# Graph-attention tail of a four-block graph network: target columns out of split rows, no masks under the logits, first tile's projection behind its transposition, first residual beside the last product

## The reference, cut to what matters

```python
def gat(x, src, dst, W, a_src, a_dst, bias, heads):       # one attention layer
    h = (x @ W).reshape(n, heads, -1)
    al_s = (h * a_src).sum(-1); al_d = (h * a_dst).sum(-1)
    e = leaky_relu(al_s[src] + al_d[dst], 0.2)
    e = exp(e - segment_max(e, dst)[dst])
    alpha = e / (segment_sum(e, dst)[dst] + 1e-16)
    return segment_sum(h[src] * alpha, dst) + bias
# block 3: h = relu(gat(h, 768 -> 4 heads x 64)); h = relu(gat(h, 256 -> 1 x 256)); h = relu(h @ Wm1 + bm1) @ Wm2 + bm2
# block 4: h = elu(gat(h, 768 -> 8 heads x 96)); h = gat(h, 768 -> 1 x 768)
x = x + block(relu(layernorm(x)))
```

## Time and profile before

| what | value |
|---|---|
| median of three runs (lowest, highest) | 935.74 us (931.85, 939.06) |
| the profiled execution, own time / span | 938.73 us / 936.9 us |
| mean granted TensorE clock | 0.949 of 2.4 GHz |
| PE, DVE, ACT, POOL busy (share of the span) | 837.0 (89%), 616.9 (66%), 378.4 (40%), 513.8 (55%) us |
| last product of block 2 ends / attention begins | 755.5 us / 764.2 us |
| last instruction of DVE ends | 933.8 us |

### The profile page before, as it was taken

How to read it: one execution, slowest core, us unless ns; L and a number is a source line. 1 busy time by engine, 2 the same in 40 slices (tenths; PEclk the granted TensorE clock), 3 DMA queues, 4 the chain that set the end, 5 groups by cost and what they waited for, 6 DMA issues and landing times.

```text
span 936.9 us, 10275 instructions
## 1 busy us (share of the span) xinstructions
PE 837.0 (89%) x4096; PEld 648.3 (69%) x4096; DVE 616.9 (66%) x700; ACT 378.4 (40%) x410; POOL 513.8 (55%) x225
## 2 busy tenths in 40 slices
PE   8999999998788999889886899999999957879877
PEld 3569966775456995666553699899879946545644
DVE  8955079899995319899998575465379563333442
ACT  1124276666643437667563343334333312110310
POOL 0437459999982738999996377166527600000000
PEclk9999999999999999999999899999999987568979
DMA  8046335344324634305322566176355360000000
GB/s 347 4 131 206 131 91 135 101 135 135 101 68 139 199 101 131 95 1 214 111 75 94 201 203 202 36 269 202 102 181 187 122 252 1 1 0 1 1 0 34
DMA packets 24263, 111.00 MB, mean 118 GB/s; under 512 B 3604, under 2 KB 5908, under 8 KB 23832
## 3 DMA queue, kind: packets, MB, share of 16 engines
q1 hardware_dynamic: 23096, 104.24, 34.1%
q10 hardware_dynamic: 1120, 6.10, 1.7%
HBM read 100.63 MB, written 0.79 MB: 108 GB/s over the span
## 4 chain that ended last, share of the span: by engine, by line
PE 57%; POOL 25%; DVE 12%; ACT 3%; issue 2%; DMA 1%; DVEq 0%; ACTq 0%
PE ps L955 20%; POOL prod L561 17%; PE ps L903 9%; POOL prod L564 6%; PE ps L940 6%; DVE prod L1685 5%; PE ps L1335 4%; POOL w_lo L549 3%; PE ps L1010 2%; PE ps L1394 2%; PE ps L1031 2%; PE ps L1311 2%; DVE qi_t L1703 1%; PE ps L1188 1%; PE ps L1329 1%
## 5 line engine op out<-in xcount | busy, mean ns | idle before, releaser
L549 POOL TENSOR_TENSOR w_lo<-w_raw,w_hi 128x1536 fp32r<-128x1536 f32 x54 | 197.0, 3655 | 146.6 <-ACT w_hi L615 146.5
L561 POOL TENSOR_TENSOR prod<-prod 128x1024 f32<-128x1024 f32 x94 | 226.5, 2425 | 40.6 <-DVE prod L1685 40.4
L720 ACT ACTIVATE prod<-ps 128x1024 f32<-128x1024 f32 x192 | 187.8, 1024 | 96.3 <-PE ps L1141 72.8
L1685 DVE TENSOR_TENSOR prod<-prod,ps 128x2048 f32<-128x2048 f32 x96 | 218.7, 2279 | 3.2 <-ACT prod L720 2.5
L1141 PE MATMUL ps<-sel_pair,h_and_q 128*128 128x512 f32 x384 | 130.7, 453 | 22.1 <-ACT prod L720 21.9
L903 PE MATMUL ps<-w_raw,h_t 128*128 128x384 f32 x408 | 141.8, 494 | 0.0
L615 ACT ACTIVATE w_hi<-w_raw 128x1536 fp32r<-128x1536 f32 x54 | 80.2, 1488 | 136.8 <-PE ps L955 93.7
L955 PE MATMUL ps<-w_hi,yt_hi 128*128 128x384 f32 x432 | 111.0, 337 | 5.2 <-POOL w_lo L549 5.2
L903 PEld LDWEIGHTS ps<-w_raw,h_t 128*128 128x128 f32 x408 | 78.2, 194 | 46.0 <-issue 2.6
L955 PE MATMUL ps<-w_lo,yt_hi 128*128 128x384 f32 x432 | 109.7, 334 | 0.0
L955 PE MATMUL ps<-w_hi,yt_lo 128*128 128x384 f32 x432 | 109.7, 334 | 0.0
(11 more groups left out here) (194 smaller groups left out, 1113.0 us busy)
## 6 DMA issues: line engine op xcount, KB each, us to landing
w_raw<-weights SPq DMA_DIRECT2D x105, 768.0 KB, 4.4
wa_in<-weights SPq DMA_DIRECT2D x6, 768.0 KB, 5.9
w_gat<-weights SPq DMA_DIRECT2D x6, 768.0 KB, 8.1
w_query<-weights SPq DMA_DIRECT2D x3, 768.0 KB, 11.3
h_and_q<-stage_hi SPq DMA_DIRECT2D x24, 96.0 KB, 2.1
h_and_q<-stage_lo SPq DMA_DIRECT2D x24, 96.0 KB, 2.2
a_vec<-gat_vectors ACTq DMA_DIRECT2D x1, 2048.0 KB, 8.0
q_t<-queries ACTq DMA_DIRECT2D x1, 1536.0 KB, 10.2
```

What stands on the lines that cost most here:

```text
L549: pool.tensor_tensor(Wl[:, j, :], raw_slab(U, 0, j), Wh[:, j, :], ALU.subtract).then_inc(w_lo_ready, 1)
L561: pool.tensor_tensor(v[:, :, 0:32], v[:, :, 0:32], v[:, :, 32:64], ALU.add).then_inc(folded_once, 1)
L720: act.activation(slot_view(s)[:, :, 32 * u:32 * u + 32], args.rearrange("p b (n l) -> p (b n) l", l=LH), ACT.Sigmoid).then_inc(sigmoid_rea ...
L1685: TT(slot_view(s), slot_view(s), ps[:, 6, o:o + L].unsqueeze(1).broadcast_to([P, NB, L]), ALU.mult).then_inc(products_ready, 1)
```

## The change

1. Columns: `logit_columns` no longer contracts over the input. It takes one product for each tile from the split rows AR[:,1] with a selector of 8 columns. It now waits for the rows (`g_dst_rows`) and stands behind `masked` on PE; DVE's copy of the columns still stands ahead of its maxima.
2. Masks: no `masks` in `logits`, and no table `noedge_s`. One 512-wide product and two of 256 columns fill each bank. `counted` takes the smaller of the weight and 1 before it multiplies by the count, in the same instruction.
3. Projection: `projection` of tile 0 (all of it in g = 0, two chunks in g = 2 and 3) goes right behind the transposition of tile 0, which for g = 0 and 2 stands ahead of that of tile 1. `keep_h` of tile 0 moves up on ACT. The last sums (L1526) run over tile 0 first and wait for each tile's `keep_h` by itself; target tile 1 goes to banks 6 and 7.
4. Residual: `last_residual(0)` starts at `out0_ready`. The `Wa` work of g = 0 is split around `norm_shift(2, 0)`, ahead of the residual of tile 1, and that of g = 1 goes behind the weights of g = 0 with a buffer of its own.

```diff
-            def logit_weights(g, w, k0, n, done):
+            def logit_weights(g, w, k0, n, done, vectors=(0, 1)):
...
-                tmp = wa_tmp[:, 0:width]
+                tmp = wa_tmp1[:] if g == 1 else wa_tmp[:, 0:width]
...
-            wait_landed(dve, 30, 0, 0)
-            logit_weights(0, raw_slab(30, 0, 0), 0, 6, True)
-            wait_landed(dve, 30, 0, 1)
-            logit_weights(1, raw_slab(30, 0, 1)[:, 0:2 * N], 0, 2, True)
-            for t in range(NT):
+            def last_residual(t):
                 wait_out(dve, LAYERS - 1, t)
                 residual(t, two_banks(2 * t)).then_inc(residual_added, 1)
                 dve.wait_ge(residual_added, t + 1)
                 norm_stats(2, t)
-            for t in range(NT):
-                norm_shift(2, t)
+            last_residual(0)
+            wait_landed(dve, 30, 0, 0)
+            logit_weights(0, raw_slab(30, 0, 0), 0, 6, False, (0,))
+            norm_shift(2, 0)
+            logit_weights(0, raw_slab(30, 0, 0), 0, 6, True, (1,))
+            last_residual(1)
+            norm_shift(2, 1)
...
             gat_weights(0)
+            wait_landed(dve, 30, 0, 1)
+            logit_weights(1, raw_slab(30, 0, 1)[:, 0:2 * N], 0, 2, True)
             heads_out(0, 0, 6, 1)
...
             def logit_columns(g):
-                hn, n = GAT[g][0], IN_CHUNKS[g]
+                hn = GAT[g][0]
+                pe.wait_ge(g_dst_rows, g + 1)
                 for t in range(NT):
-                    for k in range(n):
-                        ins = pe.matmul(ps[:, 6, t * hn:(t + 1) * hn], HT[:, k, t * P:(t + 1) * P],
-                                        Wa[:, WB[g] + k, 32:32 + hn], start=(k == 0), stop=(k == n - 1))
+                    ins = pe.matmul(ps[:, 6, t * SELK:(t + 1) * SELK], AR[:, 1, t * P:(t + 1) * P], selb[0:64, :, 0],
+                                    start=True, stop=True)
...
             def logits(g, u):
                 b0 = logit_bank(g, u)
-                masks(g, u, noedge_s, b0)
-                for i, (t, h) in enumerate(BLOCKS[g][u]):
-                    pe.matmul(block_of(b0, i), AR[:, 0, t * P:(t + 1) * P], selb[0:64, h, 0:1].broadcast_to([64, N]),
-                              start=False, stop=False)
-                    ins = pe.matmul(block_of(b0, i), selb[0:64, h, :], AR[:, 1, :], start=False, stop=(i % 2 == 1))
+                p = BLOCKS[g][u]
+                for b in range(len(p) // 2):
+                    both = ps[:, b0 + b, :].rearrange("p (h n) -> p h n", h=2)
+                    t, h = p[2 * b]
...
+                        pe.matmul(both, AR[:, 0, t * P:(t + 1) * P], selb[0:64, h:h + 2, 0:1].broadcast_to([64, 2, N]),
+                                  start=True, stop=False)
+                        for i in range(2):
+                            ins = pe.matmul(both[:, i, :], selb[0:64, h + i, :], AR[:, 1, :], start=False, stop=(i == 1))
...
-                    TT(w3, w3, c3, ALU.mult).then_inc(g_weights_ready, 1)
+                    dve.scalar_tensor_tensor(out=w3, in0=w3, scalar=1.0, in1=c3, op0=ALU.min,
+                                             op1=ALU.mult).then_inc(g_weights_ready, 1)
...
-            transposes(0, H, norm_h_ready, 0, 6, (4, 6))
-            masks(0, 0, noedge_d, 0)
-            wait_landed(pe, 30, 0, 2)
+            transpose_tile(0, H, norm_h_ready, 0, 6, 4)
...
+            pe.wait_ge(ht0_ready, 1)
+            pe.wait_ge(residual_added, 2)
+            projection(0, 0, 0, 6)
+            transpose_tile(1, H, norm_h_ready, 0, 6, 6)
+            masks(0, 0)
             logit_rows(0)
-            logit_columns(0)
             pe.wait_ge(g_src_rows, 1)
             masked(0, 0)
-            masks(0, 1, noedge_d, 4)
+            masks(0, 1)
             masked(0, 1)
-            projection(0, 0, 0, 6)
-            pe.wait_ge(g_dst_rows, 1)
+            logit_columns(0)
+            projection(0, 1, 0, 3)
             for u in range(2):
                 pe.wait_ge(g_masked_read, u + 1)
                 logits(0, u)
             max_rows(0)
-            projection(0, 1, 0, 6)
+            projection(0, 1, 3, 6)
...
+            transpose_tile(0, H, norm_h_ready, 2, 6, 4)
+            pe.wait_ge(ht0_ready, 4)
+            pe.wait_ge(w31_landed, 48)
+            projection(2, 0, 0, 2)
+            transpose_tile(1, H, norm_h_ready, 2, 6, 6)
+            projection(2, 0, 2, 3)
             logit_rows(2)
+            projection(2, 0, 3, 4)
+            pe.wait_ge(g_src_rows, 3)
+            masks(2, 0)
+            masked(2, 0)
             logit_columns(2)
...
             pe.wait_ge(g_cols_copied, 3)
-            pe.wait_ge(g_dst_rows, 3)
-            masks(2, 1, noedge_d, 6)
+            masks(2, 1)
             masked(2, 1)
-            projection(2, 0, 1, 3)
...
+            pe.wait_ge(ht0_ready, 5)
+            pe.wait_ge(w32_landed, 48)
+            projection(3, 0, 0, 2)
             logit_rows(3)
+            projection(3, 0, 2, 3)
+            pe.wait_ge(g_src_rows, 4)
+            masks(3, 0)
+            masked(3, 0)
             logit_columns(3)
...
-            pe.wait_ge(g_h_copied, 8)
...
-            for d in range(NT):
-                for u in range(2):
-                    for t in range(NT):
+            for t in range(NT):
+                pe.wait_ge(g_h_copied, 7 + t)
+                for d in range(NT):
+                    for u in range(2):
```

More of the change, by code:

```diff
@@ L846, in _ @@
             first_half(0, 4, 6, False)
+            keep_h(0, 0)
             target_rows(0)
@@ L1291, in _, with transpose_tile @@
                 layer_products(layer)
-            def transposes(e, src, ready, count, chunks, banks):
-                for t in range(NT):
[L1297 to L1300, removed]
+            def transpose_tile(t, src, ready, count, chunks, bank):
+                pe.wait_ge(ready, count + t + 1)
+                for k in range(chunks):
+                    ins = pe.transpose(chunk_tile(bank, chunks)[:, k, :], src[:, t, k * P:(k + 1) * P], ident[:])
+                ins.then_inc(t_done, 1)
             W30 = Wr[:, 0:3, :].rearrange("p j f -> p (j f)")
@@ L1341, in block_of, with masks @@
                 return ps[:, b0 + i // 2, (i % 2) * N:(i % 2 + 1) * N]
-            def masks(g, u, table, b0):
+            def masks(g, u):
                 p = BLOCKS[g][u]
+                b0 = piece_bank(g, u)
                 for b in range(len(p) // 2):
                     t = p[2 * b][0]
-                    both = table[:, g // 2, :, :] if len(BLOCKS[g]) == 1 else                         table[:, g // 2, t, :].unsqueeze(1).broadcast_to([P, 2, N])
+                    both = noedge_d[:, g // 2, :, :] if len(BLOCKS[g]) == 1 else \
+                        noedge_d[:, g // 2, t, :].unsqueeze(1).broadcast_to([P, 2, N])
                     pe.matmul(ps[:, b0 + b, :].rearrange("p (h n) -> p h n", h=2), identb[:], both, start=True, stop=False)
@@ L1359, in logits @@
                 b0 = logit_bank(g, u)
-                masks(g, u, noedge_s, b0)
-                for i, (t, h) in enumerate(BLOCKS[g][u]):
-                    pe.matmul(block_of(b0, i), AR[:, 0, t * P:(t + 1) * P], selb[0:64, h, 0:1].broadcast_to([64, N]),
-                              start=False, stop=False)
-                    ins = pe.matmul(block_of(b0, i), selb[0:64, h, :], AR[:, 1, :], start=False, stop=(i % 2 == 1))
+                p = BLOCKS[g][u]
+                for b in range(len(p) // 2):
+                    both = ps[:, b0 + b, :].rearrange("p (h n) -> p h n", h=2)
+                    t, h = p[2 * b]
+                    if len(BLOCKS[g]) == 1:
+                        pe.matmul(both, selb[0:64, h, :], AR[:, 1, :].unsqueeze(1).broadcast_to([64, 2, N]),
+                                  start=True, stop=False)
+                        for i in range(2):
+                            ins = pe.matmul(both[:, i, :], AR[:, 0, i * P:(i + 1) * P], selb[0:64, h, 0:1].broadcast_to([64, N]),
+                                            start=False, stop=(i == 1))
+                    else:
+                        pe.matmul(both, AR[:, 0, t * P:(t + 1) * P], selb[0:64, h:h + 2, 0:1].broadcast_to([64, 2, N]),
+                                  start=True, stop=False)
+                        for i in range(2):
+                            ins = pe.matmul(both[:, i, :], selb[0:64, h + i, :], AR[:, 1, :], start=False, stop=(i == 1))
                 ins.then_inc(g_logits_ready, 1)
@@ L1421, in _ @@
             weighted(0, 1, 0, 4, 2, True)
-            transposes(1, gout, gout_ready, 0, 2, (3, 7))
-            masks(1, 0, noedge_d, 4)
+            transpose_tile(0, gout, gout_ready, 0, 2, 3)
+            masks(1, 0)
+            transpose_tile(1, gout, gout_ready, 0, 2, 7)
             logit_rows(1)
-            logit_columns(1)
+            projection(1, 0, 0, 2)
             pe.wait_ge(g_src_rows, 2)
             masked(1, 0)
-            for t in range(NT):
-                projection(1, t, 0, 2)
```

(49 more changed lines are left out.)

24 lines of the change are left out of this document (11 added, 13 removed).

## The result

| | before | after |
|---|---|---|
| median of four runs each (lowest, highest), us | 937.4 (931.85, 940.91) | 912.51 (910.11, 913.43) |
| profiled execution, own time / span, us | 938.73 / 936.9 | 910.11 / 908.3 |
| mean granted clock | 0.949 | 0.962 |

The ratio is 0.9736, with a 95% interval of [0.9681, 0.9791]: 24.9 us less by the medians, 19.6 to 29.9 by the interval. The forecast was 914.3 us (905 to 924). One run of all that follow, 2202.39 us of the kernel wide_filler, was in a slower state and is left out.

A forecast was written before the change was run, and what follows sets the result against it. PE's order and its clock were taken as the bound in the tail. Gains of 5.2 + 1.8 + 5.7 + 8.7 = 21.4 us, taken from the median of 935.74, gave 914.3 us, with a range of 905 to 924.

The forecast's parts named there:

- Before attention: Part 4, from the last product to `h_t` of tile 0: copy ready at 764.2 us, against 766.6 before.
- two queues: Ahead of g = 0: ACT's copy queued behind tile 1's norm, and the wait for both residuals, hold the projection back.
- g = 0: First attention layer, projection to maxima: gain 5.2 us, with 1.5 us charged for one low-clock stretch.
- g = 1: Second layer: old columns and a mask bank go, against the new columns; gain 1.8 us.
- g = 2: Third layer: columns, masks, filled wait and low stretch gained, less new waits and transposition; gain 5.7 us.
- g = 3: Last layer: filled waits, columns, mask and clock; gain 8.7 us.
- The reason that was given for the low clock: Rows stretch of g = 3: transpositions don't count as PE activity; were they counted, 10.4 us instead of 8.7.
- Unseen costs: Minimum inside `counted` taken as nothing (1.8 us from above); new columns 0.25 us, from 0.12 each to 0.43 each.
- stages not touched: g = 1's weights and the two-layer network: no gain counted, low-clock share may shift 2 us either way.
- Only the removals pay: Rival, whole tail: only removed columns and masks gain, 12.5 us, or 923, and the moves cancel out; chance 0.22.
- the clock holds: Rival: low stretches behind the columns vanish and early projections raise the clock sooner; 28 us, 907; chance 0.15.
- The slower one: Rival: new waits turn high-clock stretches of g = 2 and 3 low, up to 40.8 us more, 955; chance 0.03.

The follow-up runs named there:

- wide_filler: Kernel before with only the new columns, plus as many unread 128-wide products where the old columns stood; 928.35 us, 0.992.
- early: Changed kernel with ACT's copy of tile 0 ahead of tile 1's norm and the projection of g = 0 in bank 0; 907.5 us, 0.9703.
- early_fill: As early, with one chunk of the second tile's projection in g = 2 moved ahead of `max_rows`; 905.38 us, 0.9675.
- run 12: Not a follow-up run: the words say that PE had executed 12 transpositions in g = 0; no kernel or measured time belongs to them.
- old_masks: Changed kernel with the second masks put back under the logits; 916.48 us, 0.9798.
- old_residual: Changed kernel with both residuals put back behind the logit weights of both layers; 915.7 us, 0.9773.
- old_order: Changed kernel with the old order of projections, ACT copies and last sums put back in all four layers; 916.71 us, 0.9794.
- the repeat: Changed kernel run again unchanged for a second trace; 912.69 us.

## Why the prediction was right

- **The bound.** PE's order and its clock, as read from the earlier trace rows. Shown for the columns by wide_filler: equal PE work, 6 us less.
- **The time is nearer than the gain, by luck.** 912.51 us is 1.8 us from the forecast. The gain was 24.9 us instead of 21.4, 3.5 more; the forecast started from 935.74 us, and a fourth run moved the median of the kernel before to 937.4.
- **Before attention.** Residual 0 at 749.5 us (forecast 749.4), the copy at 764.2 us (764.2), the rows of g = 0 at 773.3 us (772.9). That two queues keep the projection out of PE's idle time is shown by early, which changes both; neither was changed alone.
- **g = 0, 6.0 for 5.2 us.** The charged low stretch of 1.5 us didn't come; the path behind the rows took 9.0 us (8.9 at the high clock were worked out).
- **g = 1, 2.0 for 1.8 us**, from before traces that differ by 3 us among themselves.
- **g = 2, 5.1 for 5.7 us.** The price before `max_rows` is there: PE waits 0.83 us for DVE's late maxima (0.85 forecast), and early_fill gets 0.7 us of it back. That the moves of this stage pay is not shown: with the old order it took 32.4 us.
- **g = 3, 9.2 for 8.7 us.** The first projection ran at the low clock for 4.54 us, as taken, and all behind it at 1.00. The reason that was given for the low clock doesn't hold up in these traces. In the stretch from which it was read, PE also stood idle for 2.8 us ahead of the rows. In g = 0 the clock rose at 767.1 us, when PE had run 12 transpositions and begun a mask since 764.2 us. And the same projection behind the same transpositions ran at 1.00 in early_fill and in old_masks, where L1335 is the projection:

```profile
880.57 2.85 PE ps L1335 x8
```

So 4.54 us was one of several values that this projection took (3.41 us in early, 3.66 in old_residual), and that it came out as forecast is partly luck. The Trainium skill ("TensorE: Matmul & The Clock Gate", "Part 4: PE-mode transpose") says that a transposition doesn't count as PE activity for the clock; these traces don't bear that out for the transpositions of this kernel.

- **Unseen costs.** The minimum costs nothing: two operations in 2.36 us, like the two products of before. New columns: 0.12 us for both tiles, under the 0.25 taken. The row that the forecast called narrow (L1364) is 256 columns wide, with 64 partitions.
- **The mis-sized term** is the one set at zero: stages not touched. They gave 3.2 us of the mean gain of 25.5: 1.6 in the stage with the two-layer network, where the traces before differ by 4.4 us among themselves, and 1.6 in the sums of g = 2, repeatable and unexplained. With 22.3 us from the four touched stages the sum of 21.4 was 0.9 short.
- **The rivals.** "Only the removals pay" (923) lies 9.6 us above the slowest run, and old_order speaks against it; "the clock holds" was half true: all behind the columns, but not the first projections. The slower one never set in: over 25.4 us of g = 2 with the new waits the clock was 1.00.

## What to carry to other kernels

Very narrow products were paid twice here: 24 of them took as long as their weight loads, and what stood behind them ran at half the clock in most cases. Read the granted clock behind them before you price them by their own duration, and derive such columns from rows that are there already. Work moved into an idle stretch arrives only if every in-order queue on its way lets it pass: here ACT's norm of the other tile and one shared bank held it back until both were changed. Price low-clock stretches by stage and take more than one trace, as a stage that the change doesn't touch moved by 2 to 4 us here. Do the same for each part that is put back: a median of four runs doesn't tell 2 us of the part from 2 us of another stage, and the stages do.

## What the runs showed of the hardware that was not expected

A single-column power on POOL (L554, 128x1) takes 0.55 us alone, but 2.00 us at 752.03 us, while DVE runs the 1536-wide product L1799 (1.75 us); 1.99 us in the repeat and 2.00 in early. It is not DVE's work as such that stretches it: in the kernel before it took 0.55 us at 760.77 us, beside DVE's residual (L1836, 760.61 us, 0.94 us), of which one input lies in `ps`, while both inputs of L1799 lie in SBUF. The delay is hidden here, since the shift stands 3.6 us later on DVE. And 24 products with 128 columns take as long as 24 with 4 (2.88 and 2.77 us), as the weight loads of the latter do, while only the narrow ones were followed by the low clock:

```profile
771.08 2.75 PEld L1319 LDWEIGHTS ps<-w_logit,h_t 128*128 128x128 f32 x24 [0.41 <-issue]
```
